# One slot of a cross-attention and routed feed-forward kernel, its parts put in another order on four engines

## The chip, the cores and the metric

The kernel runs on one core of a Trainium2 chip. Every engine has its own program, and semaphores tie them together: TensorE (PE; its weight loads are PEld), VectorE (DVE), ScalarE (ACT), GpSimd (POOL) and SyncE (SP, which here only starts DMAs). The metric is the device time of one execution in microseconds (us); less is better.

## The reference, cut to what matters

Shapes: x and ctx are (128, 128, 256) float32: 128 batches of 128 tokens with 256 features; 16 heads of 16.

```python
def layer(x, ctx):
    q = layernorm(x) @ Wq + bq
    k, v = split(ctx @ Wkv + bkv)
    attn = softmax(q k^T / 4, axis=2)            # over the queries
    x1 = x + (attn v) @ Wo + bo
    y = layernorm(x1)
    keep = top 96 of the 128 tokens of each batch by y @ w_router
    return x1 + where(keep, gelu(y @ w_block), y)
```

## The kernel before, in words

A batch is one tile of 128 tokens by 256 features, and the main loop has one slot s per batch. In a slot each engine works on several batches at different stages, in an order written out by hand; nothing schedules it at run time but the semaphore waits. LEAD is 8. Names in the profile leave out buffer numbers, so x1_sb is shown as x_sb and rstd1 and rstd2 as rstd.

- PE, slot s: `scores(s)` (into ps_s); `transpose_inputs(s+8)` (the normalised input xhat and the context c_sb, into ps_t); `values(s-1)`; `queries_or_keys(s)`, the quarter of the queries or keys of the next four batches, into all of ps_q; `projection(s-2)`; `block_product(s-4)` into ps_t; `transpose_x1(s-3)` into the first half of ps_q; `attention(s-1)`. ps_t is shared by the input transposes and the block product, ps_q by the queries or keys and the transposed x1. So `transpose_x1(s-3)` waits until DVE has read the queries or keys of its own slot (q_raw_ready or k_ready).
- ACT: `x1_high(s-4)`, half of the last quarter of the exponentials of s-1, `attention_copy(s-2)`, the other half, `gelu_tanh(s-7)`, `inputs_high(s+8)`, and the exponentials of s in quarters 3, 2, 1.
- DVE: `x1_low(s-4)`, `maxima(s, 3)` and `(s, 2)`, `values_and_bias(s-1)`, `inputs_low(s+8)`, `inverse_sums_01(s-1)`, `maxima(s, 1)`, `queries` or `keys` (reads ps_q), `residual(s-2)`, `maxima(s, 0)`, `inverse_sums_23(s)`, `final(s-16)`, one `stats` of a pair (the input's in even slots, x1's in odd ones), `product_scaled(s-4)` (reads ps_t). The `router` steps for a group of eight batches lie in five slots of eight.
- POOL: `normalise(s+9)`, in odd slots `rstd1_of_pair(s+11)`, in even slots `rstd2_of_pair(s-4)`, `gelu_square(s-5)`, `values_over_sums(s-1)` (needs `inverse_sums_01(s-1)`, gives v_pad to the attention), `scale_and_shift` in one slot of eight, `unprocessed(s-16)` (gives u_ready to DVE's `final(s-16)`), then `gelu_factor`, `gelu_sum`, `input_and_bias`, `gelu_cubic`, `gelu_product`.

The two waits that the prediction speaks of most are these, one on PE and one on DVE:

```python
# transpose_x1(b), slot = b + 3, quad = slot // 4 * 4 + 4
pe.wait_ge((q_raw_ready, k_ready)[slot % 4 // 2], quad + 2 + slot % 2 * 2)
# final(b), for a batch whose unprocessed part POOL makes
dve.wait_ge(u_ready, b + 1 - u_on_act(b))
```

Of the kernel before, what the change touches and what calls it, by code (L numbers as in the profile page):

```python
# [6 lines left out]
def cross_attention_routed_ffn(  # L7
# [43 lines left out]
    with ctx:  # L51
# [93 lines left out]
        def has(b):  # L145
            return 0 <= b < B

        def upto(b):
            return min(b + 1, B)
# [83 lines left out]
        def _(sp):  # L233
# [63 lines left out]
            load_c(6)  # L297
            load_x(10)
            load_x(12)
            load_x(14)  # L300
            load_c(8)
            load_c(10)
            queries_even_odd_of_pair(2)
            load_c(12)
            load_c(14)
            queries_even_odd_of_pair(4)
            load_x(16)
            queries_even_odd_of_pair(6)

            for s in range(3, B + 18):  # L310
# [12 lines left out]
        def _(pe):  # L323
# [73 lines left out]
            def transpose_inputs(b, settled=False):  # L397

                if not has(b):
                    return  # L400
                if not settled:
                    inputs_ready(b)
                if has(b - LEAD - 5):
                    pe.wait_ge(z_ready, upto(b - LEAD - 5))
                elif 2 <= b <= 4:
                    pe.wait_ge(t_lo_ready, upto(b - 2))
                elif b > 4:
                    pe.wait_ge(t_lo_ready, upto(b - 1))
# [63 lines left out]
            def block_product(b, settled=False):  # L472

                if not has(b):
                    return
                if not settled:
                    pe.wait_ge(xt_ready, upto(b))
                pe.wait_ge(t_lo_ready, upto(b + LEAD + 4))
                if has(b - 1) and not has(b + LEAD + 4):
                    pe.wait_ge(z_ready, upto(b - 1))  # L480
                if b == 0:
                    pe.wait_ge(w_z_lo_ready, 1)
                three_terms(ps_z,
                            lambda a, c: (xt_hi, xt_lo)[a][:, b % 2, c * T:(c + 1) * T],
                            lambda a, c: (w_z_hi, w_z_lo)[a][:, c, :]).then_inc(z_mm, 1)
# [81 lines left out]
            for s in range(2, B - 1):  # L567
                sure = 20 <= s < B - 8
                scores(s)
                if s < 4:  # L570
                    transpose_inputs(2 * s + 4)
                else:
                    transpose_inputs(s + LEAD, s > 4)
                values(s - 1)
                if s < 4:
                    queries_or_keys_of_pair(2 * s, 1)
                else:
                    queries_or_keys(s)
                keep_columns(s - 16)
                candidates(s - 12)  # L580
                projection(s - 2, sure)
                queries_and_keys_ready(s + 1)
                if s < 4:
                    transpose_inputs(2 * s + 5)
                if s == 2:
                    queries_or_keys_of_pair(6, 0)
                if s >= 4:
                    inputs_ready(s + LEAD + 1)
                block_product(s - 4, sure)
                if sure:  # L590
                    scaled_values_ready(s - 1)
                transpose_x1(s - 3, sure)
                router_bank_free(s + 1)
                attention(s - 1, sure)

            scores(B - 1)
            values(B - 2)
            projection(B - 3)
            block_product(B - 5)
            transpose_x1(B - 4)  # L600
            values(B - 1)
            attention(B - 2)
# [15 lines left out]
        def _(act):  # L618
# [108 lines left out]
            for s in range(2, B):  # L727
                sure = 20 <= s < B - 1
                x1_high(s - 4, sure)
                exps(s - 1, 0, halves=(0,))  # L730
                attention_copy(s - 2, sure)
                exps(s - 1, 0, halves=(1,))
                gelu_tanh(s - 7)
                inputs_high(s + LEAD if s >= 4 else 2 * s + 4)
                exps(s, 3, sure)
                exps(s, 2)
                if s < 4:
                    inputs_high(2 * s + 5)
                exps(s, 1)
                if s == 2:  # L740
                    block_weights_high()
# [29 lines left out]
        def _(dve):  # L771
# [156 lines left out]
                        dve.wait_ge(v_pad_ready, upto(b - 2))  # L928
                    nc.vector.tensor_tensor(v_sb[:, b % 2, :], ps_v, bv_sb[:, :], ALU.add).then_inc(v_ready, 1)  # L929

            def product_scaled(b, settled=False):

                if has(b):
                    dve.wait_ge(z_mm, upto(b))
                    if not settled:
                        dve.wait_ge(rstd2_ready, upto(b))
# [96 lines left out]
            for s in range(2, B):  # L1033
                sure = 20 <= s < B - 1
                x1_low(s - 4)
                if s == 3:
                    block_weights_low()
                router(s - 13, 2)
                router(s - 14, 4)
                router(s - 15, 6)  # L1040
                router(s - 16, 8)
                maxima(s, 3)
                maxima(s, 2)
                router(s - 16, 9)
                values_and_bias(s - 1, sure)
                inputs_low(s + LEAD if s >= 4 else 2 * s + 4)
                inverse_sums_01(s - 1)
                maxima(s, 1)
                if s < 4:
                    keys_of_pair(2 * s)  # L1050
# [8 lines left out]
                if s < 4:  # L1059
                    inputs_low(2 * s + 5)  # L1060
                if s == 2:
                    queries_of_pair(6)
                if s == B - 1:
                    values_and_bias(B - 1)
                router(s - 12, 1)
                router(s - 13, 3)
                router(s - 14, 5)
                router(s - 15, 7)
                inverse_sums_23(s)
                final(s - 16, sure)  # L1070
                stats2_of_pair(s - 3)
                if s >= 4:
                    stats1_of_pair(s + 12)
                product_scaled(s - 4, sure)
                if s < 4:
                    stats1_of_pair(2 * s + 8)

# [41 lines left out]
        def _(pool):  # L1119
# [9 lines left out]
            nc.gpsimd.memset(q_eo[:, 1, :, :, :, :], 0.0).then_inc(q_eo_zero, 1)  # L1129

            def rstd1_of_pair(b):

# [125 lines left out]
            normalise(5)  # L1258
            input_and_bias(0)
            input_and_bias(1)  # L1260
            rstd1_of_pair(6)
            normalise(6)
            normalise(7)
# [6 lines left out]
            for s in range(2, 4):  # L1270
# [5 lines left out]
            rstd1_of_pair(14)  # L1276

            for s in range(4, B):
                sure = 20 <= s < B - 1
                normalise(s + LEAD + 1, sure)  # L1280
                rstd1_of_pair(s + 11)
                rstd2_of_pair(s - 4)
                gelu_square(s - 5, sure)
                values_over_sums(s - 1, sure)
                scale_and_shift(s - 16)
                unprocessed(s - 16, sure)
                gelu_factor(s - 5)
                gelu_sum(s - 7)
                input_and_bias(s + 2)
                gelu_cubic(s - 5)  # L1290
                gelu_product(s - 7)

            rstd2_of_pair(B - 4)
            gelu_factor(B - 5)
            scale_and_shift(B - 16)
            values_over_sums(B - 1)
# [41 lines left out]
```

## Time and profile before

| | |
|---|---|
| time, median of 3 runs | 902.11 us (901.8 to 902.36) |
| the profiled execution: its own time, its span | 904.1 us, 902.3 us |
| busy share of the span: PE, PEld | 96%, 80% |
| DVE, ACT, POOL | 95%, 96%, 88% |
| granted clock of TensorE, mean | 0.991 of full speed (2.4 GHz) |
| DMA | 70.40 MB, mean 78 GB/s |

The busy shares are taken over the whole span, with a start and an end that are less full than the middle. The durations in the timeline reach from an instruction's start to its end and overlap with the next one's; what an instruction costs its engine is the distance from its start to the next start. Below that is called its spacing.

### The profile page before, as it was taken

The numbers are of one execution on the slowest core, as the hardware profiler recorded it, in microseconds if no ns is written. First come the engines' busy times: TensorE is split into PE (matmuls) and PEld (weight loads), VectorE is DVE, ScalarE is ACT, GpSimd is POOL, SyncE is SP. The second block draws the span as 40 slices with busy tenths as digits, with TensorE's granted clock in tenths as the row PEclk, the third lists the DMA queues.
The fourth block names the chain that finished last, engine by engine and source line by source line (L and its number), as shares of the span: only waits on it lengthen the run. The fifth ranks groups of instructions, "written<-read, shape, count | busy, mean of one in ns | idle before, by whom it ended". The sixth has DMA issues, their size and how long they took to land. (4 is left out here: it accounts for less than half of the span.)

```text
span 902.3 us, 30174 instructions
## 1 busy us (share of the span) xinstructions
PE 864.8 (96%) x9842; PEld 718.8 (80%) x9842; DVE 857.9 (95%) x2068; ACT 870.6 (96%) x4632; POOL 789.6 (88%) x1489
## 2 busy tenths in 40 slices
PE   6999999999999999999999999999999999999972
PEld 6778888888888888888888888888888888888752
DVE  5888999999999999999999999999999999999987
ACT  4999999999999999999999999999999999999984
POOL 5468879999999999999999999999999999998865
PEclk9999999999999999999999999999999999999997
DMA  7221123232323232223333222323222323211102
GB/s 233 69 65 53 54 63 86 79 93 59 84 82 89 72 96 69 79 79 85 84 83 91 57 80 88 91 72 95 61 85 79 87 78 90 75 40 40 41 24 94
DMA packets 71357, 70.40 MB, mean 78 GB/s; under 512 B 12064, under 2 KB 63520, under 8 KB 71200
## 3 DMA queue, kind: packets, MB, share of 16 engines
q1 hardware_dynamic: 69840, 67.68, 26.4%
q8 instruction: 79, 1.29, 0.6%
q10 hardware_dynamic: 1360, 0.79, 0.3%
q14 instruction: 78, 0.64, 0.2%
HBM read 35.13 MB, written 16.78 MB: 58 GB/s over the span
## 5 line engine op out<-in xcount | busy, mean ns | idle before, releaser
L646 ACT ACTIVATE e_sb<-ps_s,neg_max 128x128 f32<-128x128 f32 x2048 | 772.1, 639 | 2.8 <-DVE neg_max L805 2.7
L646 ACT ACTIVATION_READ_ACCUMULATOR e_sb<-ps_s,neg_max 128x1 f32 x2048 | 718.2, 464 | 0.0
L805 DVE TENSOR_REDUCE neg_max<-ps_s 128x4 f32<-128x512 f32 x512 | 331.0, 666 | 19.7 <-PE ps_s L385 18.2
L385 PE MATMUL ps_s<-q_eo,k_sb 32*128 32x256 f32 x2048 | 146.6, 399 | 3.6 <-ACT e_sb L646 1.5
L450 PE MATMUL ps_a<-e_sb,v_pad 128*32 128x128 f32 x4096 | 138.4, 276 | 1.5 <-POOL v_pad L1168 0.9
L344 PE MATMUL ps_a<-w_o_sb,o_sb 128*128 128x256 f32 x512 | 131.7, 379 | 4.0 <-DVE v_sb L929 3.8
L450 PEld LDWEIGHTS ps_a<-e_sb,v_pad 128*32 128x32 f32 x4096 | 104.1, 109 | 23.2 <-issue 21.5
L385 PEld LDWEIGHTS ps_s<-q_eo,k_sb 32*128 32x128 f32 x2048 | 95.8, 184 | 32.9 <-issue 28.7
L344 PEld LDWEIGHTS ps_a<-w_o_sb,o_sb 128*128 128x128 f32 x512 | 93.8, 189 | 22.8 <-issue 4.7
L1157 POOL TENSOR_TENSOR x_sb<-x_sb,bo_sb 128x256 f32<-128x256 f32 x128 | 105.1, 822 | 0.2
L1168 POOL TENSOR_TENSOR v_pad<-v_sb,recip 128x256 f32<-128x256 f32 x128 | 79.5, 621 | 29.1 <-DVE recip L865 27.1
L657 ACT CAST t_hi<-ps_t 128x512 fp32r<-128x512 f32 x126 | 94.3, 748 | 7.5 <-PE ps_t L414 7.0
L688 ACT ACTIVATE g_sb<-g_sb 128x256 f32<-128x256 f32 x128 | 99.0, 774 | 1.4 <-POOL g_sb L1215 1.4
L337 PE MATMUL ps_t<-w_z_hi,xt_hi 128*128 128x258 f32 x256 | 96.4, 377 | 2.2 <-DVE z_sb L941 2.2
L665 ACT COPY o_sb<-ps_a 128x256 f32<-128x256 f32 x128 | 91.1, 712 | 2.4 <-PE ps_a L450 2.4
L633 ACT CAST xt_hi<-ps_q 128x256 fp32r<-128x256 f32 x128 | 88.4, 691 | 1.4 <-PE ps_q L430 1.4
L1215 POOL TENSOR_TENSOR g_sb<-g_sb,z_sb 128x256 f32<-128x256 f32 x128 | 88.3, 690 | 0.3
L873 DVE TENSOR_TENSOR t_lo<-ps_t,t_hi 128x512 fp32r<-128x512 f32 x126 | 85.2, 676 | 2.7 <-ACT t_hi L657 2.6
L337 PE MATMUL ps_a<-w_v_hi,t_hi 128*128 128x256 f32 x256 | 83.2, 325 | 0.7 <-DVE w_z_sb L797 0.7
L1229 POOL TENSOR_TENSOR z_sb<-g_sb,z_sb 128x256 f32<-128x256 f32 x121 | 82.8, 684 | 0.0
L1198 POOL TENSOR_TENSOR g_sb<-z_sb 128x256 f32<-128x256 f32 x123 | 75.3, 612 | 0.0
L337 PE MATMUL ps_a<-w_v_lo,t_hi 128*128 128x256 f32 x256 | 72.5, 283 | 0.0
(113 smaller groups left out, 2213.8 us busy)
## 6 DMA issues: line engine op xcount, KB each, us to landing
x_sb<-in_x SPq DMA_DIRECT2D x64, 256.0 KB, 3.0
c_sb<-in_ctx SPq DMA_DIRECT2D x64, 256.0 KB, 3.0
out<-z_sb SPq DMA_DIRECT2D x64, 256.0 KB, 2.4
q_eo<-q_raw SPq DMA_DIRECT2D x504, 32.0 KB, 2.0
z_sb<-in_L_xattn_Wkv ACTq DMA_DIRECT2D x2, 256.0 KB, 6.7
z_sb<-in_L_xattn_Wq ACTq DMA_DIRECT2D x1, 256.0 KB, 3.6
w_z_sb<-in_L_ffn_w_block SPq DMA_DIRECT2D x1, 256.0 KB, 8.0
w_o_sb<-in_L_xattn_Wo SPq DMA_DIRECT2D x1, 256.0 KB, 7.1
```

The source lines that it names most:

```text
L337: last = nc.tensor.matmul(dst, lhs(a, c), rhs(b, c), start=(c == 0 and n == 0), stop=(c == C - 1 and n == len(terms) - 1))
L344: last = nc.tensor.matmul(dst, lhs(c), rhs(c), start=(c == 0), stop=(c == C - 1))
L385: mm = nc.tensor.matmul(ps_s[:, bank(b, j), c, :, :], k_sb[rows, r2, c, h * T:(h + 1) * T], q_eo[rows, r2, :, c, h, :], start=True, stop=True)
L450: mm = nc.tensor.matmul(ps_attn[32 * j:32 * j + 32, c * T:(c + 1) * T], v_pad[:, b % 2, c * J + j, par:par + 2, :].rearrange("p a d -> p ( ...
L633: nc.scalar.copy(xt_hi[:, b % 2, :], ps_xt).then_inc(xt_hi_ready, 1)
L646: last = nc.scalar.activation(e_sb[:, b % 3, j, c, par, :], ps_s[:, bank(b, j), c, par, :], ACT.Exp, bias=neg_max[:, b % 4, h:h + 1], accu ...
L657: nc.scalar.copy(t_hi[:, n, :, :, h * T:(h + 1) * T].rearrange("p k c t -> p (k c) t"), inputs_bank(b)[:, :].rearrange("p (n t) -> p n t", ...
L665: nc.scalar.copy(o_sb[:, b % 2, :], ps_attn).then_inc(o_ready, 1)
L688: nc.scalar.activation(g_sb[:, b % 4, :], g_sb[:, b % 4, :], ACT.Tanh, scale=SLOPE).then_inc(tanh_ready, 1)
L805: nc.vector.tensor_reduce(neg_max[:, b % 4, :].rearrange("p (c j q) -> p j c q", c=C, j=J)[:, j, :, :], ps_s[:, bank(b, j), :, :, :], AX.X ...
L1157: nc.gpsimd.tensor_tensor(x_sb[:, b % RX, :], x_sb[:, b % RX, :], bo_sb[:, :], ALU.add).then_inc(xb_ready, 1)
L1215: nc.gpsimd.tensor_tensor(g_sb[:, b % 4, :], g_sb[:, b % 4, :], z_sb[:, b % R, 0:E], ALU.mult).then_inc(cubic_ready, 1)
```

## The change: what it does

It moves parts within the slot, and adds or removes no arithmetic.

- PE: `transpose_inputs(s+8)` goes from behind the scores to behind `transpose_x1(s-3)`, and `block_product(s-4)` from there to behind the values. Their two waits for the shared ps_t are moved on by one batch.
- ACT: `inputs_high` is now that of batch s+7, behind `x1_high`; the last quarter of the exponentials of s-1 is no longer cut in two by the attention's copy.
- DVE: `inputs_low(s+7)` behind `x1_low`; `product_scaled(s-4)` behind `inverse_sums_01(s-1)`.
- POOL: `values_over_sums(s-1)` is first. `rstd1_of_pair` is now in even slots, and `rstd2_of_pair` is in odd ones, behind `input_and_bias`.
- At the start SP waits for one weight before four of its loads and puts two x loads later, a memset of POOL comes later, and in the last slots the block product has its new place as well.

```diff
@@ the PE loop
                 scores(s)
                 if s < 4:
                     transpose_inputs(2 * s + 4)
-                else:
-                    transpose_inputs(s + LEAD, s > 4)
                 values(s - 1)
+                block_product(s - 4, sure)
...
                 projection(s - 2, sure)
                 queries_and_keys_ready(s + 1)
-                if s < 4:
-                    transpose_inputs(2 * s + 5)
+                if s >= 4:
+                    inputs_ready(s + LEAD)
+                transpose_x1(s - 3, sure)
+                transpose_inputs(s + LEAD if s >= 4 else 2 * s + 5, s >= 4)
+                router_bank_free(s + 1)
+                attention(s - 1)
...
-                block_product(s - 4, sure)
-                if sure:
-                    scaled_values_ready(s - 1)
-                transpose_x1(s - 3, sure)
-                router_bank_free(s + 1)
-                attention(s - 1, sure)
@@ its waits
-                if has(b - LEAD - 5):
-                    pe.wait_ge(z_ready, upto(b - LEAD - 5))
+                if has(b - LEAD - 4):
+                    pe.wait_ge(z_ready, upto(b - LEAD - 4))
...
-                pe.wait_ge(t_lo_ready, upto(b + LEAD + 4))
+                pe.wait_ge(t_lo_ready, upto(b + LEAD + 3))
@@ the ACT loop
                 x1_high(s - 4, sure)
-                exps(s - 1, 0, halves=(0,))
+                if s == 3:
+                    inputs_high(9)
+                elif s >= 4:
+                    inputs_high(s + LEAD - 1)
                 attention_copy(s - 2, sure)
-                exps(s - 1, 0, halves=(1,))
+                exps(s - 1, 0)
                 gelu_tanh(s - 7)
-                inputs_high(s + LEAD if s >= 4 else 2 * s + 4)
@@ the DVE loop
                 x1_low(s - 4)
...
+                elif s >= 4:
+                    inputs_low(s + LEAD - 1)
...
                 values_and_bias(s - 1, sure)
-                inputs_low(s + LEAD if s >= 4 else 2 * s + 4)
...
                 inverse_sums_01(s - 1)
+                product_scaled(s - 4)
...
-                product_scaled(s - 4, sure)
@@ the POOL loop
+                values_over_sums(s - 1, sure)
                 normalise(s + LEAD + 1, sure)
-                rstd1_of_pair(s + 11)
-                rstd2_of_pair(s - 4)
+                rstd1_of_pair(s + 10)
                 gelu_square(s - 5, sure)
-                values_over_sums(s - 1, sure)
                 scale_and_shift(s - 16)
                 unprocessed(s - 16, sure)
                 gelu_factor(s - 5)
                 gelu_sum(s - 7)
                 input_and_bias(s + 2)
+                rstd2_of_pair(s - 3)
```

PE, one slot of the middle of the program, the first matmul of each group and what it waits for (the rest of a group stands behind it). First before:

```order
L385 MATMUL ps_s<-q_eo,k_sb 128x256 [waits exp_ready1,recip_23_ready]
L414 MATMUL ps_t<-ident,xhat 128x128 [waits z_ready]
L337 MATMUL ps_a<-w_v_hi,t_hi 128x256 [waits o_ready]
L337 MATMUL ps_q<-t_hi,w_k_hi 128x512 [waits xt_ready]
L344 MATMUL ps_a<-w_o_sb,o_sb 128x256 [waits v_ready]
L337 MATMUL ps_t<-w_z_hi,xt_hi 128x258 [waits c_in6,t_lo_ready,xhat_ready,q_eo_in1]
L430 MATMUL ps_q<-ident,x1_sb 128x128 [waits k_ready,v_pad_ready]
L450 MATMUL ps_a<-e_sb,v_pad 32x128 [waits x1_ready]
```

And the same slot of the change:

```order
L386 MATMUL ps_s<-q_eo,k_sb 128x256 [waits exp_ready1,recip_23_ready]
L338 MATMUL ps_a<-w_v_hi,t_hi 128x256 [waits o_ready]
L338 MATMUL ps_t<-w_z_hi,xt_hi 128x258 [waits t_lo_ready]
L338 MATMUL ps_q<-t_hi,w_k_hi 128x512 [waits xt_ready]
L345 MATMUL ps_a<-w_o_sb,o_sb 128x256 [waits v_ready]
L431 MATMUL ps_q<-ident,x1_sb 128x128 [waits k_ready,xhat_ready,q_eo_in1]
L415 MATMUL ps_t<-ident,xhat 128x128 [waits z_ready]
L451 MATMUL ps_a<-e_sb,v_pad 32x128 [waits x1_ready,v_pad_ready]
```

The block product (ps_t with w_z) has left the place between the projection (w_o) and the transposed x1, whose first matmul waits for k_ready.

POOL, from the scaled values (v_pad, L1168) to the unprocessed part (x_sb with alpha and beta, L1247) in two slots running, before:

```order
L1168 TENSOR_TENSOR v_pad<-v_sb,recip 128x8x2x16 [waits recip_ready]
L1247 TENSOR_SCALAR x_sb<-x_sb,alpha,beta 128x256 [waits beta_ready]
L1208 TENSOR_SCALAR g_sb<-g_sb 128x256 [waits square_ready]
L1222 TENSOR_SCALAR g_sb<-g_sb 128x256 [waits tanh_ready]
L1157 TENSOR_TENSOR x_sb<-x_sb,bo_sb 128x256 [waits xhat_ready]
```

And of the change, in an even slot:

```order
L1166 TENSOR_TENSOR v_pad<-v_sb,recip 128x8x2x16 [waits recip_ready]
L1146 TENSOR_SCALAR xhat<-x_sb,neg_m,rstd 128x256 [waits rstd1_r]
L1134 TENSOR_SCALAR ve<-st 128x2 [waits st1_r]
L1135 TENSOR_SCALAR neg_m<-st 128x2
L1137 TENSOR_TENSOR rstd<-ve,minus_half 128x2 [waits ve1_r]
L1196 TENSOR_TENSOR g_sb<-z_sb 128x256 [waits z_ready]
L1245 TENSOR_SCALAR x_sb<-x_sb,alpha,beta 128x256 [waits beta_ready]
L1206 TENSOR_SCALAR g_sb<-g_sb 128x256 [waits square_ready]
```

The normalised input, three small operations and the square now lie between the scaled values and the unprocessed part, which nothing separated before.

## Rows read from the trace of the kernel before

**Rows 1.** Busy time by engine in 80 us of the middle (busy, instructions; TensorE clock, DMA)

```profile
480.00:560.00 80.00, 79.66 (x915) 66.29 (x914) 79.20 (x199) 80.00 (x434) 75.07 (x141) 1.00 0.28 81
```

**Rows 2.** Timeline of PE, scores of slots 16 and 120: start, us, engine, line, operation

```profile
128.02 1.15 PE L385 MATMUL ps_s<-q_eo,k_sb 32*128 32x256 f32 x16
...
823.82 1.15 PE L385 MATMUL ps_s<-q_eo,k_sb 32*128 32x256 f32 x16
```

**Rows 3.** Timeline of PE, slot 6: scores, last keys, block product, transposed x1, next scores

```profile
61.47 1.15 PE L385 MATMUL ps_s<-q_eo,k_sb 32*128 32x256 f32 x16
...
64.91 0.39 PE L337 MATMUL ps_q<-t_lo,w_k_hi 128*128 128x512 f32 x1
...
65.81 0.47 PE L337 MATMUL ps_t<-w_z_hi,xt_hi 128*128 128x258 f32 x1
66.12 0.28 PE L337 MATMUL ps_t<-w_z_hi,xt_lo 128*128 128x258 f32 x1
...
66.72 0.38 PE L430 MATMUL ps_q<-ident,x_sb 128*128 128x128 f32 x2
...
68.04 1.15 PE L385 MATMUL ps_s<-q_eo,k_sb 32*128 32x256 f32 x16
```

**Rows 4.** Timeline of PE and of DVE: queries in slot 3, and who waited for them

```profile
39.15 0.28 PE L337 MATMUL ps_q<-t_lo,w_q_hi 128*128 128x256 f32 x1
...
39.53 0.69 DVE L886 TENSOR_TENSOR q_raw<-ps_q,bq_sb 128x512 f32<-128x512 f32 x1 [0.17 <-PE ps_q L337]
```

**Rows 5.** Timeline of DVE, from one final to the next and a later one

```profile
509.10 0.72 DVE L994 SCALAR_TENSOR_TENSOR z_sb<-z_sb,half_keep,x_sb 128x256 f32<-128x256 f32 x1
509.74 0.69 DVE L851 BATCH_NORM_STATS2 st<-x_sb 128x6 f32<-128x512 f32 x1
510.36 0.46 DVE L941 TENSOR_SCALAR z_sb<-ps_t,rstd 128x258 f32<-128x258 f32 x1
510.74 0.41 DVE L818 TENSOR_TENSOR xt_lo<-ps_q,xt_hi 128x256 fp32r<-128x256 f32 x1
511.07 1.27 DVE L805 TENSOR_REDUCE neg_max<-ps_s 128x4 f32<-128x512 f32 x2
...
513.23 0.19 DVE L865 RECIPROCAL recip<-sums 128x8 f32<-128x8 f32 x1
...
513.90 0.74 DVE L910 TENSOR_SCALAR q_raw<-ps_q,bq_sb 128x512 f32<-128x512 f32 x1
...
515.60 0.63 DVE L994 SCALAR_TENSOR_TENSOR z_sb<-z_sb,half_keep,x_sb 128x256 f32<-128x256 f32 x1
...
522.17 0.51 DVE L994 SCALAR_TENSOR_TENSOR z_sb<-z_sb,half_keep,x_sb 128x256 f32<-128x256 f32 x1
522.60 0.69 DVE L851 BATCH_NORM_STATS2 st<-x_sb 128x6 f32<-128x512 f32 x1
```

**Rows 6.** Timeline of POOL, around the unprocessed part (L1247) of two slots

```profile
508.03 0.21 POOL L1237 TENSOR_TENSOR beta<-drop_rstd,st 128x8 f32<-128x8 f32 x1 [0.61 <-DVE half_keep L978]
...
508.51 0.55 POOL L1247 TENSOR_SCALAR x_sb<-x_sb,alpha,beta 128x256 f32<-128x256 f32 x1
509.14 0.40 POOL L1208 TENSOR_SCALAR g_sb<-g_sb 128x256 f32<-128x256 f32 x1
...
511.96 0.56 POOL L1148 TENSOR_SCALAR xhat<-x_sb,neg_m,rstd 128x256 f32<-128x256 f32 x1
512.60 0.19 POOL L1136 TENSOR_SCALAR ve<-st 128x2 f32<-128x2 f32 x1
...
513.73 0.61 POOL L1198 TENSOR_TENSOR g_sb<-z_sb 128x256 f32<-128x256 f32 x1
...
514.91 0.56 POOL L1247 TENSOR_SCALAR x_sb<-x_sb,alpha,beta 128x256 f32<-128x256 f32 x1
```

**Rows 7.** Groups by line of DVE, the router's rounds: count, busy us, mean ns

```profile
L967 DVE MAX8 top<-cand 8x8 f32<-8x128 f32 x64 | 17.5, 273 | 0.4
L961 DVE MATCH_REPLACE8 cand<-top,cand 8x128 f32<-8x128 f32 x64 | 16.9, 264 | 0.0
```

More of the change, by code:

```diff
@@ L299, in _ @@
             load_x(12)
-            load_x(14)
+            sp.wait_ge(w_in["v"], 16)
             load_c(8)
@@ L303, in _ @@
             queries_even_odd_of_pair(2)
+            load_x(14)
+            queries_even_odd_of_pair(4)
             load_c(12)
+            load_x(16)
             load_c(14)
-            queries_even_odd_of_pair(4)
-            load_x(16)
             queries_even_odd_of_pair(6)
@@ L477, in block_product @@
                     pe.wait_ge(xt_ready, upto(b))
-                pe.wait_ge(t_lo_ready, upto(b + LEAD + 4))
-                if has(b - 1) and not has(b + LEAD + 4):
+                pe.wait_ge(t_lo_ready, upto(b + LEAD + 3))
+                if has(b - 1) and not has(b + LEAD + 3):
                     pe.wait_ge(z_ready, upto(b - 1))
@@ L582, in _ @@
                 queries_and_keys_ready(s + 1)
-                if s < 4:
-                    transpose_inputs(2 * s + 5)
+                if s >= 4:
[4 more added lines that the diff above has]
+                attention(s - 1)
                 if s == 2:
                     queries_or_keys_of_pair(6, 0)
-                if s >= 4:
-                    inputs_ready(s + LEAD + 1)
-                block_product(s - 4, sure)
-                if sure:
-                    scaled_values_ready(s - 1)
-                transpose_x1(s - 3, sure)
-                router_bank_free(s + 1)
-                attention(s - 1, sure)
             scores(B - 1)
             values(B - 2)
+            block_product(B - 5)
             projection(B - 3)
-            block_product(B - 5)
             transpose_x1(B - 4)
@@ L729, in _ @@
                 x1_high(s - 4, sure)
-                exps(s - 1, 0, halves=(0,))
+                if s == 3:
+                    inputs_high(9)
+                elif s >= 4:
+                    inputs_high(s + LEAD - 1)
                 attention_copy(s - 2, sure)
-                exps(s - 1, 0, halves=(1,))
+                exps(s - 1, 0)
                 gelu_tanh(s - 7)
-                inputs_high(s + LEAD if s >= 4 else 2 * s + 4)
+                if s < 4:
+                    inputs_high(2 * s + 4)
                 exps(s, 3, sure)
                 exps(s, 2)
-                if s < 4:
-                    inputs_high(2 * s + 5)
                 exps(s, 1)
@@ L929, in values_and_bias, with product_scaled @@
                     nc.vector.tensor_tensor(v_sb[:, b % 2, :], ps_v, bv_sb[:, :], ALU.add).then_inc(v_ready, 1)
-            def product_scaled(b, settled=False):
+            def product_scaled(b):
                 if has(b):
                     dve.wait_ge(z_mm, upto(b))
-                    if not settled:
-                        dve.wait_ge(rstd2_ready, upto(b))
+                    dve.wait_ge(rstd2_ready, upto(b))
                     if b % 2 == 0 and has(b - R):
@@ L1037, in _ @@
                     block_weights_low()
+                    inputs_low(9)
+                elif s >= 4:
+                    inputs_low(s + LEAD - 1)
                 router(s - 13, 2)
@@ L1045, in _ @@
                 values_and_bias(s - 1, sure)
-                inputs_low(s + LEAD if s >= 4 else 2 * s + 4)
+                if s < 4:
+                    inputs_low(2 * s + 4)
                 inverse_sums_01(s - 1)
+                product_scaled(s - 4)
                 maxima(s, 1)
@@ L1058, in _ @@
                 maxima(s, 0)
-                if s < 4:
-                    inputs_low(2 * s + 5)
                 if s == 2:
@@ L1128, in _ @@
             nc.gpsimd.memset(q_eo[:, 0, :, :, 2:4, :], 0.0).then_inc(q_eo_zero, 1)
-            nc.gpsimd.memset(q_eo[:, 1, :, :, :, :], 0.0).then_inc(q_eo_zero, 1)
             def rstd1_of_pair(b):
@@ L1260, in _ @@
             input_and_bias(1)
+            nc.gpsimd.memset(q_eo[:, 1, :, :, :, :], 0.0).then_inc(q_eo_zero, 1)
             rstd1_of_pair(6)
@@ L1275, in _ @@
                 input_and_bias(s + 2)
-            rstd1_of_pair(14)
+            rstd2_of_pair(0)
             for s in range(4, B):
                 sure = 20 <= s < B - 1
+                values_over_sums(s - 1, sure)
                 normalise(s + LEAD + 1, sure)
-                rstd1_of_pair(s + 11)
-                rstd2_of_pair(s - 4)
+                rstd1_of_pair(s + 10)
                 gelu_square(s - 5, sure)
-                values_over_sums(s - 1, sure)
                 scale_and_shift(s - 16)
@@ L1289, in _ @@
                 input_and_bias(s + 2)
+                rstd2_of_pair(s - 3)
                 gelu_cubic(s - 5)
                 gelu_product(s - 7)
-            rstd2_of_pair(B - 4)
             gelu_factor(B - 5)
```

## The prediction

> **What bounds the kernel now.** I read the busy time of a stretch in the middle first. ACT is busy all 80.00 of 80 us, PE 79.66, DVE 79.20 and POOL 75.07 [rows 1]: four engines within 7% of each other, so a gain on one can't pass the next, while a wait put on any of them can soon be a loss. Then the pace. From the scores of slot 16 to those of slot 120 it takes 695.80 us [rows 2], 104 slots or 13 rounds of eight (the router's period): 6.69 us a slot, 53.52 a round. With ACT never idle, that is ACT's work. Slot 6, early, before ACT has all of its work, takes 6.57 [rows 3], with PE's matmuls end to end: that is PE's own need. For DVE I added spacings along one slot, and found that it is nearly as full as ACT (below). So the question to ask of each moved part is which wait it puts on PE, DVE or POOL, and not what it saves.
>
> **PE: the block product.** It now stands behind the values. It opened with a matmul 0.31 us from its second, where its others stand 0.12 apart [rows 3]; behind the values, which are of the same kind, I expect 0.12, a saving of 0 to 0.19. But it also was the cover of a wait. The transposed x1 goes into ps_q, and must let DVE read the queries or keys there first. Before, it started 1.81 us behind the last matmul of the keys; the block product began at 0.90 [rows 3], and there the transposed x1 stands now. What it needs: the matmul's 0.39, then 0.10 until DVE starts (39.43 to 39.53 [rows 4]), DVE's 0.74 [rows 5], and a handover for which I take POOL to DVE, 0.04 (509.06 to 509.10 [rows 5, 6]): 1.27. So PE stands still for 0.37 in each slot with queries or keys, even when DVE is there in time. PE's slot becomes 6.57 + 0.37 - 0.19 = 6.75, or 6.94 if nothing is saved. The moved input transposes cost what they did, as far as any row tells. I take 6.85, the middle: already above ACT's 6.69.
>
> **POOL and DVE: the unprocessed part.** This is the larger term. DVE's final of a batch needs POOL's unprocessed part. Before, that stood directly behind the scaled values. Now the normalised input, in even slots the three operations of its statistic, and the square come between. I count from DVE's reciprocal that the scaled values need.
> - POOL's way in an even slot: the reciprocal's 0.19 [rows 5] and a handover of 0.04; normalised input and statistic 1.77 (511.96 to 513.73); square and scaled values 1.18 (513.73 to 514.91); the unprocessed part 0.56 [rows 6]; a handover of 0.04. Sum 3.78.
> - DVE's way to the same final: reciprocal and maxima 0.67 (513.23 to 513.90), the scaled product, now here, 0.38 (510.36 to 510.74), then queries, residual, maxima and reciprocal 1.70 (513.90 to 515.60) [rows 5]. Sum 2.75. So DVE stands at final for 1.03 us. The wait for the queries' matmuls lies inside this stretch and is hidden by it: PE's 6.85 leaves DVE 0.56 to wait at most, by DVE's 6.29 below.
> - From final to the next slot's reciprocal: final itself; statistics 0.62; x1's low half 0.33; then two maxima, values and the inputs' low half 2.16 (511.07 to 513.23) [rows 5]. That is 3.11 besides final.
>
> Final took 0.64 where it started right behind the unprocessed part, 0.04 before POOL's next operation (509.10 against 509.14), and 0.43 in a later slot [rows 5, 6]. In the even slots of the change each final starts right behind the unprocessed part, so 0.64 is the row nearest to it. The Trainium skill (SBUF — State Buffer, Who interferes with whom) says that a VectorE instruction with two SBUF inputs and a GpSimd instruction that reads SBUF can't run together: the later one waits. By that rule the 0.64 is what every such meeting costs, and the rows agree with it; if all finals took 0.43 instead, the sum below would be 11 us less.
>
> An even slot is then 3.78 + 0.64 + 3.11 = 7.53 us on DVE. An odd slot has no such wait: without the statistic's 1.13 (512.60 to 513.73 [rows 6]) POOL needs 2.65, less than DVE's 2.75. It is 2.75 + 0.43 + 3.11 = 6.29, or 6.50 with a slow final; I take 6.4. Who waits for a late DVE: PE, whose next transposed x1 needs the queries read, and ACT, whose exponentials need the maxima. So the pair costs 13.93 where PE alone would allow 13.70, and a round 55.7.
>
> Two more things lie on this way. The router's rounds, 17.5 + 16.9 us for 16 groups [rows 7], are 2.15 a round of eight slots. The two of its MAX8 that stand between reciprocal and final in even slots vanish in the wait (2 x 0.27), so 1.6 counts. And beta and alpha, once a round and in an even slot, add 0.48 ahead of the unprocessed part (508.03 to 508.51 [rows 6]). A round is 55.7 + 1.6 + 0.5 = 57.8 against 53.52: **4.3 us more, and 56 over 13 rounds.** In the other 16 slots with queries or keys (4 to 15, no unprocessed part yet, and 120 to 123) I count PE's 6.85 against some 6.65: 3 us.
>
> **What costs nothing.** ACT's converted inputs are now made at the start of the slot from transposes that stand a whole attention ahead of it, so its wait there goes; but ACT was busy all the time [rows 1], and what is late next is DVE. The exponentials joined into one quarter are the same instructions. The scaled product earlier on DVE is counted above; PE's input transposes no longer wait for it last. The scaled values' first place on POOL brings nothing, since their reciprocal decides, and the attention that needs them comes last in PE's slot. x1's statistic, now late in odd slots, is wanted a slot later. The start (SP's wait for a weight, two loads issued later, a memset moved) I bound by 2 us either way, some 0.12 a slot, the 6.69 less 6.57 of rows 2 and 3, for 16 slots, and take at nothing.
>
> **The sum.** 56 + 3 = 59. The profiled execution took 904.1 us with a span of 902.3, and stands 2.0 above the median of 902.1. The difference goes onto the median: 902 + 59 = 961.
>
> **The rivals.**
> - *PE's wait alone.* If POOL's unprocessed part is in time after all, because POOL starts its slot earlier or DVE arrives later by itself, the slot is PE's 6.85: 120 slots x 0.16 = 19 us, 921; with 6.94, 932. For it: only a second of the two engines has to be 1.03 us off my count. Against it: the count is made of plain spacings.
> - *The waits add up.* If DVE's wait for the queries isn't covered by POOL's way, because the reciprocal moves with it, each even slot costs up to 0.56 more: 13 x 4 x 0.56 = 29 us, 990. Against it: the reciprocal stands ahead of the queries.
> - *Not slower.* PE saves 0.19 and its transposes no longer stand behind DVE's scaled product. If DVE's read of the queries ended within the 0.90 that are left, and final met no wait, ACT's 6.69 would go on bounding the slot, and with a smoother start the time is 900 to 902. The point that decides is a way through DVE of 0.90 where I count 1.27, and 2.75 for POOL where I count 3.78. Faster by more than 2 us it can't be, since ACT is full.
>
> **How the numbers follow.** The forecast, 940 to 980, gets 0.60. PE's wait alone gets 0.18, the added waits above 980 get 0.12. Not slower gets 0.10, half of it within 0.2% (about what a measurement of this kernel tells from no change), half of it faster. The range goes from 921, PE's wait alone at its middle, to 980; it leaves out the case that isn't slower, most of the added waits and a little of the second case, some 0.2 together. So faster 0.05, same 0.05, slower 0.90.
>
> **What would show it.** In the profile after, ACT should be busy less than 95% of the middle. DVE's final should wait for POOL's unprocessed part by about 1 us in even slots, most in the one with beta. PE's transposed x1 should wait for DVE's queries or keys in every slot. The scores should stand some 57.8 us apart over eight slots, uneven, with slots of 6.4 to 6.9 after slots of 7.5 and more. The forecast is wrong if ACT is still full, if final shows no wait, or if the transposed x1 starts within 1 us of the last keys' matmul.

## The result, and the profile after

The changed kernel takes **967.11 us** (median of 4 runs, 965.74 to 967.82), the kernel before 902.24 (901.8 to 902.62): a ratio of 1.0717, 95% interval 1.0699 to 1.0736. The forecast was 961 with a range of 921 to 980, so sign and size came out. The profiled execution took 965.74 us with a span of 963.9, 61.6 more than the span of before.

Busy time of the same 80 us as in [rows 1] (PE, PEld, DVE, ACT, POOL, with the number of instructions; then TensorE's clock, DMA share, GB/s):

```profile
480.00:560.00 80.00, 76.16 (x839) 59.58 (x838) 74.06 (x173) 74.29 (x396) 68.59 (x132) 1.00 0.28 77
```

ACT fell from 80.00 to 74.29, and every other engine fell with it. No engine took over as the bound: all of them now wait. The clock is granted in full, so nothing of the loss lies there.

The scores of slots 16 and 120 in the timeline of PE, as in [rows 2]:

```profile
129.43 1.15 PE L386 MATMUL ps_s<-q_eo,k_sb 32*128 32x256 f32 x16
...
884.20 1.15 PE L386 MATMUL ps_s<-q_eo,k_sb 32*128 32x256 f32 x16
```

They are 754.77 us apart, 58.06 a round, where it was 695.80 and 53.52. So 58.97 of the 61.6 us were lost in these 104 slots. Slots 4 to 15 lost another 3.43 (83.14 against 79.71 from the scores of slot 4 to those of slot 16), and the rest about cancels: the profiled execution starts 2.8 sooner, and slots 0 to 3 and 120 to 127 take some 2 more.

Who waits, from the table of waits between 200 and 760 us (engine, what it wrote, who released it: us in total, times, longest):

```profile
POOL v_pad L1166 <- DVE recip L863: 52.0, 47, 1.4
ACT e_sb L642 <- DVE neg_max L803: 28.0, 38, 1.2
...
DVE z_sb L991 <- POOL x_sb L1245: 21.4, 37, 1.3
...
PEld ps_t L338 <- DVE t_lo L871: 15.5, 37, 1.0
```

Read the third row shown first: DVE's final (L991) waits for POOL's unprocessed part (L1245). DVE is late after that, so POOL waits for the next reciprocal (L863) and ACT for the maxima (L803). The same table of the kernel before, which goes down to sums of 0.9 us, has none of these three.

One even slot without the router's shift on DVE, from reciprocal to reciprocal, with what POOL does in it (start, us, engine, line, operation, and in brackets the idle time before and its releaser):

```profile
554.36 0.19 DVE L863 RECIPROCAL recip<-sums 128x8 f32<-128x8 f32 x1
...
555.77 0.75 DVE L916 TENSOR_SCALAR k_sb<-ps_q,bk_sb 128x512 f32<-128x512 f32 x1 [0.27 <-issue]
...
558.20 0.72 DVE L991 SCALAR_TENSOR_TENSOR z_sb<-z_sb,half_keep,x_sb 128x256 f32<-128x256 f32 x1 [0.49 <-POOL x_sb L1245]
...
561.90 0.19 DVE L863 RECIPROCAL recip<-sums 128x8 f32<-128x8 f32 x1
```

```profile
554.63 0.62 POOL L1166 TENSOR_TENSOR v_pad<-v_sb,recip 128x256 f32<-128x256 f32 x1
555.24 0.55 POOL L1146 TENSOR_SCALAR xhat<-x_sb,neg_m,rstd 128x256 f32<-128x256 f32 x1
...
556.33 0.71 POOL L1137 TENSOR_TENSOR rstd<-ve,minus_half 128x2 f32<-128x2 f32 x1
557.01 0.61 POOL L1196 TENSOR_TENSOR g_sb<-z_sb 128x256 f32<-128x256 f32 x1
557.61 0.56 POOL L1245 TENSOR_SCALAR x_sb<-x_sb,alpha,beta 128x256 f32<-128x256 f32 x1
558.25 0.41 POOL L1206 TENSOR_SCALAR g_sb<-g_sb 128x256 f32<-128x256 f32 x1
```

From reciprocal to final it is 3.84 us; POOL fills this with the values, the normalised input, the statistic, the square and the unprocessed part, without a gap worth naming. The slot is 7.54 (554.36 to 561.90). Final waits 0.49 of it. That is less than the 1 us that the prediction named as a sign, because DVE has waited for PE on the way there (0.27 for the keys in the row of L916, some 0.15 at the projection), a wait that the prediction had placed inside this stretch.

The odd slot before it, from reciprocal to reciprocal (547.76 to 554.36), and PE's projection in it:

```profile
547.76 0.19 DVE L863 RECIPROCAL recip<-sums 128x8 f32<-128x8 f32 x1
...
549.65 0.42 DVE L825 TENSOR_TENSOR x_sb<-ps_a,x_sb 128x256 f32<-128x256 f32 x1
...
550.71 0.43 DVE L991 SCALAR_TENSOR_TENSOR z_sb<-z_sb,half_keep,x_sb 128x256 f32<-128x256 f32 x1
...
552.82 1.29 DVE L803 TENSOR_REDUCE neg_max<-ps_s 128x4 f32<-128x512 f32 x2
```

```profile
548.59 1.02 PE L345 MATMUL ps_a<-w_o_sb,o_sb 128*128 128x256 f32 x4
```

It takes 6.60: 2.95 to final, 0.35 for final, 3.30 to the next reciprocal. Final waits for nothing here. But DVE follows PE at two places: the residual (L825) starts right behind the projection (549.61), and the maxima (L803) start behind the scores' matmuls, which end at 552.68.

And PE's slot 6, as in [rows 3], before the router starts:

```profile
60.15 1.15 PE L386 MATMUL ps_s<-q_eo,k_sb 32*128 32x256 f32 x16
...
62.04 0.28 PE L338 MATMUL ps_t<-w_z_hi,xt_hi 128*128 128x258 f32 x1
62.16 0.28 PE L338 MATMUL ps_t<-w_z_hi,xt_lo 128*128 128x258 f32 x1
...
63.91 0.39 PE L338 MATMUL ps_q<-t_lo,w_k_hi 128*128 128x512 f32 x1
...
65.29 0.41 PE L431 MATMUL ps_q<-ident,x_sb 128*128 128x128 f32 x2
...
67.08 1.15 PE L386 MATMUL ps_s<-q_eo,k_sb 32*128 32x256 f32 x16
```

The block product now opens with the plain distance of 0.12, so its 0.19 is saved. The transposed x1 starts 1.38 behind the start of the last matmul of the keys, though nothing of PE's lies there but the projection. The slot is 6.93, and it was 6.57.

### The profile page after: what moved, and what is told of

Read it like the earlier page. It is cut to its first block and busy times, and to the rows that moved or that the text cites. A ratio compares the mean times of both kernels' runs of the same rounds, so it can differ in the third digit from the quotient of the medians.

```text
span 963.9 us, 30180 instructions
## 1 busy us (share of the span) xinstructions
PE 899.5 (93%) x9842; PEld 706.8 (73%) x9842; DVE 882.2 (92%) x2068; ACT 882.4 (92%) x4632; POOL 785.1 (81%) x1489
## 5 line engine op out<-in xcount | busy, mean ns | idle before, releaser
L642 ACT ACTIVATE e_sb<-ps_s,neg_max 128x128 f32<-128x128 f32 x2048 | 692.6, 444 | 39.9 <-DVE neg_max L803 39.5
L642 ACT ACTIVATION_READ_ACCUMULATOR e_sb<-ps_s,neg_max 128x1 f32 x2048 | 540.3, 269 | 0.0
L803 DVE TENSOR_REDUCE neg_max<-ps_s 128x4 f32<-128x512 f32 x512 | 336.1, 676 | 12.1 <-PE ps_s L386 8.1
L386 PEld LDWEIGHTS ps_s<-q_eo,k_sb 32*128 32x128 f32 x2048 | 92.9, 184 | 31.2 <-issue 24.1
L991 DVE SCALAR_TENSOR_TENSOR z_sb<-z_sb,half_keep,x_sb 128x256 f32<-128x256 f32 x128 | 71.9, 566 | 31.4 <-POOL x_sb L1245 31.1
L1155 POOL TENSOR_TENSOR x_sb<-x_sb,bo_sb 128x256 f32<-128x256 f32 x128 | 92.8, 725 | 0.2
L338 PE MATMUL ps_t<-w_z_hi,xt_hi 128*128 128x258 f32 x256 | 78.2, 305 | 13.7 <-DVE t_lo L871 10.5
L338 PEld LDWEIGHTS ps_a<-w_v_hi,t_hi 128*128 128x128 f32 x256 | 48.1, 188 | 42.5 <-issue 42.0
L431 PEld LDWEIGHTS ps_q<-ident,x_sb 128*128 128x128 f32 x256 | 26.0, 140 | 67.5 <-issue 43.4
L431 PE MATMUL ps_q<-ident,x_sb 128*128 128x128 f32 x256 | 52.4, 286 | 21.7 <-DVE q_raw L908 7.9
```

Of the source, the lines that this page charges most:

```text
L338: last = nc.tensor.matmul(dst, lhs(a, c), rhs(b, c), start=(c == 0 and n == 0), stop=(c == C - 1 and n == len(terms) - 1))
L386: mm = nc.tensor.matmul(ps_s[:, bank(b, j), c, :, :], k_sb[rows, r2, c, h * T:(h + 1) * T], q_eo[rows, r2, :, c, h, :], start=True, stop=True)
L642: last = nc.scalar.activation(e_sb[:, b % 3, j, c, par, :], ps_s[:, bank(b, j), c, par, :], ACT.Exp, bias=neg_max[:, b % 4, h:h + 1], accu ...
L803: nc.vector.tensor_reduce(neg_max[:, b % 4, :].rearrange("p (c j q) -> p j c q", c=C, j=J)[:, j, :, :], ps_s[:, bank(b, j), :, :, :], AX.X ...
L1155: nc.gpsimd.tensor_tensor(x_sb[:, b % RX, :], x_sb[:, b % RX, :], bo_sb[:, :], ALU.add).then_inc(xb_ready, 1)
```

## The experiments

Each kernel was timed against the kernel before on the same chip (903.45 us for the first four, 902.11 for the last three). "Round" is the distance of the scores of slots 16 and 120 divided by 13, as above.

### POOL's unprocessed part directly behind the values

```diff
                 values_over_sums(s - 1, sure)
+                scale_and_shift(s - 16)
+                unprocessed(s - 16, sure)
                 normalise(s + LEAD + 1, sure)
...
                 gelu_square(s - 5, sure)
-                scale_and_shift(s - 16)
-                unprocessed(s - 16, sure)
```

> The changed kernel, but GpSimd does the router's scale and shift and the unprocessed sum directly behind the values, ahead of the normalising, the square root and the square. Theory (GpSimd's order makes most of the loss): the final sum's wait of 0.5 us in plain even slots and 1.3 us in those with the router's shift goes; what is left is TensorE's slot of 6.92 us, so a round of eight falls from 58.2 to some 55.5 us and the time from 967 to about 930 us (918 to 942). Rival (GpSimd's order is harmless and TensorE's order and VectorE's moved work make the loss): within 3 us of 967.

Measured: 939.0 us, ratio 1.0391 (1.0376 to 1.0407), inside the theory's range. The round is 55.87. The waits for the same stretch of time, those that speak of POOL, DVE and PE:

```profile
PEld ps_q L431 <- issue: 33.5, 63, 0.8
...
POOL v_pad L1166 <- DVE recip L863: 9.4, 27, 0.9
```

Final's wait for the unprocessed part is gone from the table, ACT's for the maxima too, and so is PE's for `t_lo`. POOL's order is shown to cost 28 us, 13 rounds of 2.19. What is left is a slot of 6.92 to 6.96 in seven of the eight places of a round (the eighth takes 7.3): PE's, with the transposed x1 standing still. That is the first row; "issue" means that the view names no releaser.

### PE's inputs ahead of x1

```diff
-                transpose_x1(s - 3, sure)
                 transpose_inputs(s + LEAD if s >= 4 else 2 * s + 5, s >= 4)
                 router_bank_free(s + 1)
+                transpose_x1(s - 3, sure)
```

> The changed kernel, but TensorE transposes the inputs of a later item ahead of x1 instead of behind it, so that some 0.57 us of its own work lies between the last keys or queries and the transpose that waits for VectorE to read them. Theory (two separate costs, TensorE's wait of 0.3 to 0.4 us per slot and GpSimd's order in even slots): the slots that now take 6.92 us fall to about 6.6, the even slots stay bound by the unprocessed sum, so the time falls by 5 to 15 us, to 952 to 962. Rival (TensorE's wait sets every slot): eight times 0.3 us per round, about 2.4 us in each of 15 rounds, to about 930.

Measured: 963.34 us, ratio 1.066 (1.0645 to 1.0676), just above the theory's 962 and far from the rival's 930. Slots 4 to 15 fell from 6.92 to between 6.63 and 6.75, which gives 3.4 us (from the scores of slot 4 to those of slot 16, 79.76 against 83.14). But the round is 57.98 against 58.06: where the unprocessed part exists, the edit is worth next to nothing. Its rows show why, from one reciprocal of an odd slot to the next of an even one, and that one's final:

```profile
545.05 0.18 DVE L863 RECIPROCAL recip<-sums 128x8 f32<-128x8 f32 x1
...
551.39 0.19 DVE L863 RECIPROCAL recip<-sums 128x8 f32<-128x8 f32 x1
...
555.44 0.72 DVE L991 SCALAR_TENSOR_TENSOR z_sb<-z_sb,half_keep,x_sb 128x256 f32<-128x256 f32 x1 [0.76 <-POOL x_sb L1245]
```

```profile
551.17 0.74 POOL L1227 TENSOR_TENSOR z_sb<-g_sb,z_sb 128x256 f32<-128x256 f32 x1
551.86 0.62 POOL L1166 TENSOR_TENSOR v_pad<-v_sb,recip 128x256 f32<-128x256 f32 x1
```

The odd slot is 6.34 now instead of 6.60. But at 551.39 POOL is still at the last operation of the odd slot, so the values start 0.47 behind the reciprocal instead of 0.27, and final comes after 4.05 instead of 3.84. What PE and DVE gain in the odd slot, POOL's own work takes back in the even one. The loop is POOL's odd slot, its even slot as far as the unprocessed part, and DVE from final to the next reciprocal; PE has no part in it. So it goes in two of a round's four pairs of slots. In the other two the odd slot holds steps of the router, takes 6.6 and 7.2 in both kernels, and has nothing to gain.

### Both

The two edits above together.

> Both edits at once: GpSimd's unprocessed sum directly behind the values and TensorE's inputs ahead of x1. Theory: neither wait is left, the slot is ScalarE's or TensorE's 6.6 to 6.7 us as in the kernel before, and the earlier start of 2 us is kept: 897 to 906 us. Rival (a third cost lies in VectorE's own moved work, the scaled product ahead of the maxima and the low parts of the inputs early in the slot): 910 to 930.

Measured: 916.95 us, ratio 1.0154 (1.0138 to 1.0171), in the rival's range. The round is 54.47. The edit on PE, worth 3.8 us alone, is worth 22 once the unprocessed part is early (939.0 to 916.95). So the two waits don't add up: PE's is hidden as long as POOL's is there. Still 13.5 us are missing to the kernel before. Busy time in the middle, as in [rows 1]:

```profile
480.00:560.00 80.00, 79.73 (x908) 65.39 (x907) 79.29 (x192) 79.25 (x424) 74.35 (x140) 1.00 0.29 81
```

DVE is busy 79.29 of 80, for a round that is 0.95 longer than before: its instructions take longer from start to start. But not those that the rival names: the scaled product takes 433 ns in the mean against 461 before, and the low half of the inputs 673 against 675. Two groups of DVE between 200 and 760 us, before and in this kernel (busy us, mean ns | idle before):

```profile
L994 DVE SCALAR_TENSOR_TENSOR z_sb<-z_sb,half_keep,x_sb 128x256 f32<-128x256 f32 x84 | 41.5, 494 | 1.1
L972 DVE TENSOR_SCALAR keep_row<-cand 8x128 f32<-8x128 f32 x10 | 2.1, 208 | 0.0
```

```profile
L991 DVE SCALAR_TENSOR_TENSOR z_sb<-z_sb,half_keep,x_sb 128x256 f32<-128x256 f32 x82 | 45.5, 555 | 2.2
L969 DVE TENSOR_SCALAR keep_row<-cand 8x128 f32<-8x128 f32 x10 | 4.6, 462 | 0.0
```

Eight finals a round at 61 ns more are 0.49, one keep_row is 0.25: 0.74 of the 0.95. Both are longer by whatever POOL runs beside them (see the last section). By the distances from start to next start, without the idle time that the view lists, the two make 0.64 a round between the scores of slots 16 and 120. The rest moved both ways: the maxima take 0.54 more, queries and keys 0.45, the reciprocals 0.25; the scaled product and x1's low half take 0.57 less, and listed idle time fell by 0.40. So the 0.95 is a balance, and the longer finals are its cause only as far as these rows tell: no run took them away. Nor did a run test the rival that the waits of this kernel offer: POOL now stands 1.1 once a round for the router's half_keep (10.8 us between 200 and 760 us, 5.5 before), and PE's attention then waits for the values (3.3 us).

### POOL's order alone, in the kernel before

```diff
             for s in range(4, B):
                 sure = 20 <= s < B - 1
+                values_over_sums(s - 1, sure)
                 normalise(s + LEAD + 1, sure)
-                rstd1_of_pair(s + 11)
-                rstd2_of_pair(s - 4)
+                rstd1_of_pair(s + 10)
                 gelu_square(s - 5, sure)
-                values_over_sums(s - 1, sure)
...
                 input_and_bias(s + 2)
+                rstd2_of_pair(s - 3)
```

The statistics ahead of the loop and behind it move along, and DVE's scaled product now waits for x1's statistic by itself, as in the change; no such wait shows in its table.

> The kernel before, with the changed kernel's order of GpSimd alone: values first, then the normalising, the square roots and the square, and only then the unprocessed sum. Theory (GpSimd's order makes most of the loss): the final sum on VectorE waits in the even slots and the round grows from 53.5 to 57 to 60.5 us, 945 to 995 us. Rival (the order is harmless where TensorE and VectorE keep theirs): 902, within 3 us.

Measured: 1006.22 us, ratio 1.1139 (1.1123 to 1.1156), outside what either theory said: more than the whole change costs. The round is 61.15. An even slot with the router's shift, on DVE, and who stands behind it on PE, ACT and POOL:

```profile
568.24 0.72 DVE L994 SCALAR_TENSOR_TENSOR z_sb<-z_sb,half_keep,x_sb 128x256 f32<-128x256 f32 x1 [1.71 <-POOL x_sb L1247]
```

```profile
570.02 0.44 PE L414 MATMUL ps_t<-ident,xhat 128*128 128x128 f32 x2 [1.29 <-DVE z_sb L941]
```

```profile
570.71 0.59 ACT L657 CAST t_hi<-ps_t 128x512 fp32r<-128x512 f32 x1 [1.61 <-PE ps_t L414]
```

```profile
572.64 0.62 POOL L1168 TENSOR_TENSOR v_pad<-v_sb,recip 128x256 f32<-128x256 f32 x1 [1.53 <-DVE recip L865]
```

In the old order DVE's scaled product stands behind final, PE's input transposes stand right behind the scores and wait for it, and ACT waits for those. So a late final passes through DVE, PE and ACT on its way back to POOL. With the change's other moves (the scaled product early on DVE, the transposes late on PE) the same order of POOL gives 967. So they are worth 39 us where final is late; where it is in time, as in the first kernel above, they come with PE's wait and leave the kernel 36 us above the kernel before.

This kernel also bears on the start. Its loads are those of the kernel before, and its first scores stand at 15.07 us; with the change's start they stand at 14.53 in the change and at 14.90 to 15.29 in the six other kernels here, and in the profiled execution of before at 17.29. So most of the 2.8 us by which the change seems to start sooner isn't the change's.

### The old order of the normalising, with the new rest

```diff
-                values_over_sums(s - 1, sure)
                 normalise(s + LEAD + 1, sure)
                 rstd1_of_pair(s + 10)
                 gelu_square(s - 5, sure)
+                values_over_sums(s - 1, sure)
                 scale_and_shift(s - 16)
```

> The changed kernel, but GpSimd does the normalising, the square root and the square ahead of the values, as in the kernel before; TensorE's and VectorE's new orders stay. Theory (what costs is work of GpSimd between the values and the unprocessed sum): the same gain as with the unprocessed sum directly behind the values, so slots of 6.92 us throughout, set by TensorE's wait for the keys or queries to be read: 930 to 940. Rival (the place of the values early in GpSimd's slot also matters, for the attention or for the normalising): over 945 or under 925.

Measured: 943.94 us, ratio 1.046 (1.0442 to 1.0478); the round is 56.32. The theory's upper end was 940, and the runs lie above it, just below the rival's 945. Then the same with PE's inputs ahead of x1, the edit shown for the second kernel:

> The same, and TensorE transposes the inputs ahead of x1. Theory (with the unprocessed sum directly behind the values TensorE set 6.93 us a slot, without the waits VectorE is full and sets 54.5 us a round, 1.0 over the kernel before, some of it because the final sum took 0.9 us beside GpSimd's square): with the square gone from beside the final sum the round comes to 53.6 to 54.2, the time to 904 to 914. Rival (VectorE's own order costs the 1.0 us): 915 to 919, as with both edits before.

Measured: 940.7 us, ratio 1.0424 (1.0409 to 1.044); the round is 56.25. A miss for both theories. The waits of this second kernel, in the same stretch:

```profile
POOL ve L1177 <- DVE st L832: 41.2, 39, 1.1
...
PE ps_a L451 <- POOL v_pad L1166: 18.9, 40, 0.6
DVE z_sb L991 <- POOL x_sb L1245: 17.3, 40, 0.8
```

The first of them is new. The change has moved the statistic of x1 into the odd slot, behind `input_and_bias`. It needs what DVE computes behind its final of the same slot; in the kernel before it stood a slot later. With the values behind the normalising and the square, POOL gets to it about 1 us before DVE does, stands there, and starts its even slot late; final waits again, 40 times (20 times in the first of the two kernels). So, by these waits, POOL is again in the loop in both kernels, and with it PE's edit is again worth nothing in the round (56.25 against 56.32).

### POOL's neighbour of final

```diff
                 unprocessed(s - 16, sure)
+                input_and_bias(s + 2)
                 gelu_factor(s - 5)
                 gelu_sum(s - 7)
-                input_and_bias(s + 2)
                 rstd2_of_pair(s - 3)
```

> The changed kernel, but GpSimd adds the bias to a later input directly behind the unprocessed sum, and does the gelu's factor and sum behind that. Theory (the even slots are a chain through the unprocessed sum and the final sum, and the final sum takes 0.64 us instead of 0.42 because of the neighbour on GpSimd): the final sum takes 0.42 us everywhere and the round falls by three or four times 0.2 us, so 955 to 960. Rival (the neighbour does not set it, or the 0.2 us are given back in the next wait): within 3 us of 967.

Measured: 978.41 us, ratio 1.0841 (1.0825 to 1.0858); the round is 58.98. A miss for both, with the other sign than the theory's: the neighbour does set final's time, but this one makes it longer. An even slot of this kernel, on POOL and on DVE:

```profile
520.27 0.56 POOL L1245 TENSOR_SCALAR x_sb<-x_sb,alpha,beta 128x256 f32<-128x256 f32 x1
520.79 0.73 POOL L1155 TENSOR_TENSOR x_sb<-x_sb,bo_sb 128x256 f32<-128x256 f32 x1
```

```profile
520.86 0.94 DVE L991 SCALAR_TENSOR_TENSOR z_sb<-z_sb,half_keep,x_sb 128x256 f32<-128x256 f32 x1 [0.17 <-POOL x_sb L1245]
```

Final starts 0.07 behind POOL's next operation and ends 0.28 after that one's end (521.52 to 521.80). In the change the neighbour is shorter (0.41), and final takes 0.72. Four finals a round at 0.22 more are 0.88, and the round grew by 0.92. In the kernel before the same neighbour did no harm, as these rows show:

```profile
482.32 1.01 POOL L1157 TENSOR_TENSOR x_sb<-x_sb,bo_sb 128x256 f32<-128x256 f32 x1
```

```profile
482.33 0.42 DVE L994 SCALAR_TENSOR_TENSOR z_sb<-z_sb,half_keep,x_sb 128x256 f32<-128x256 f32 x1
```

There it was final that went through, and POOL's operation that took 1.01 instead of 0.73. I had taken the 0.42 for a property of the neighbour; it belongs to the one of the two that goes first.

## Why the prediction was right, point by point

**What bounds it.** Four engines within 7% of each other, so that a wait put on one becomes a loss: so it was. ACT is busy 93% of the middle.

**PE.** The saving of 0.19 came in full. The way through DVE, taken as 1.27, is 1.38 in slot 6: DVE's read of the keys starts at 64.40 and takes 0.75, so what I had too small is the handover from DVE to PE, 0.14 where I took POOL's to DVE of 0.04. So PE stands 0.48 and not 0.37. Another 0.07 came on top, nearly all of it in the moved input transposes and the transposed x1, 0.78 together where they took 0.72; I had put that at nothing. The slot is 6.93. With the whole saving my own sum was 6.75, so that 6.85 is so near is partly the luck of having taken the middle. For the slots outside the routed stretch I counted 3 us; slots 4 to 15 alone gave 3.43.

**POOL and DVE.** The way to final in an even slot is 3.84 (taken 3.78) and with the router's shift 4.28 (3.78 + 0.48). Final's spacing is 0.65 (558.20 to the statistics at 558.85; taken 0.64), and from its end to the next reciprocal it is 3.05 (taken 3.11). The even slot is 7.54, and I had 7.53. The term that was too small is the odd slot: 6.60 where I took 6.4. I had DVE's waits for PE hidden. In the odd slot they stand in the open: 2.95 to final instead of 2.75, most of it at the projection, and 3.30 behind final instead of 3.11, at the scores. Final itself was short, 0.35 where I took 0.43 to 0.64. With PE's inputs ahead of x1 only the wait at the scores goes, and the odd slot is 2.93 + 0.35 + 3.06 (545.05 to 551.39); that this comes near my 6.29 is luck. The router and its shift add some 1.5 a round to four pairs of 14.14, where I took 2.1: part of its steps fill DVE's waits for PE in the odd slots too. So a round is 58.06 against the 57.8 of the text because 0.8 too little in the odd slots stands against 0.6 too much for the router. 13 rounds cost 59.0 instead of 56.

**The sum.** 59 was forecast. The spans differ by 61.6, the medians by 64.9. The profiled execution of before stands 1.9 over the median of 902.24, that of after 1.4 under its own, which accounts for the 3.3 between the two. Of the 5.9 us between 59 and 64.9, 3 lie in the rounds; 1.9 in the slots outside them that I counted with 3 (3.43 in slots 4 to 15, 1.43 in slots 120 to 123); 0.7 in the first four slots, which I had taken at nothing.

**What I did not name.** PE's block product, now early in the slot, waits for DVE's low half of the inputs: 0.8 us at its longest on PE. It is a consequence of the late final: the wait is absent where the unprocessed part is early (the first and the third kernel).

**The rivals.** "PE's wait alone" (921 to 932) is what the kernel with the early unprocessed part shows, at 939, 7 us above its range: the mechanism is there and worth 22 us, but it lies below the larger one. "The waits add up" is excluded for the even slots, where DVE's wait for the keys lies inside the 3.84, and by the second and third kernels: the waits overlap. In the odd slots a part of DVE's waits for PE did show, as said. "Not slower" would have needed both ways to be shorter, and with both shortened the kernel still takes 917.

**Where the cause is shown and where argued.** That POOL's order costs 28 us, and PE's wait another 22 below it, is shown by taking each away. The 13.5 that are left are only read from the rows of DVE, and their cause stays open. The moves of ACT, of DVE and of the start were not tried by themselves.

## What to carry to other kernels

Where two engines hand work back and forth, follow the loop: here unprocessed part, final, next reciprocal, next values. An operation put ahead of the one that another engine waits for lengthens that way by its full duration, and costs what the other engine's own way doesn't cover: the 2.37 us put ahead of the unprocessed part in an even slot (555.24 to 557.61) left final a wait of 0.49. And everything outside the loop can be improved nearly without effect until the loop is cut. So take the longest wait away first, and judge a second edit only on top of that: the same move on TensorE was worth 4 us before and 22 after. And an order of one engine belongs to the orders of the others: POOL's alone in the old kernel cost 103 us, together with the change's other moves 65.

## What the hardware showed that I had not expected

I expected that final is slowed by a fixed 0.2 us beside some of POOL's operations. The rows read as if one of the two waits out the other whole. Where final is the one that waits, it ends 0.26 to 0.30 us behind the end of POOL's operation: 0.72 beside one of 0.41, 0.94 beside one of 0.73. Two operations of POOL in a row can be waited out together. The kernel with both edits, on POOL and on DVE:

```profile
480.05 0.56 POOL L1146 TENSOR_SCALAR xhat<-x_sb,neg_m,rstd 128x256 f32<-128x256 f32 x1
480.57 0.62 POOL L1196 TENSOR_TENSOR g_sb<-z_sb 128x256 f32<-128x256 f32 x1
```

```profile
480.55 0.92 DVE L991 SCALAR_TENSOR_TENSOR z_sb<-z_sb,half_keep,x_sb 128x256 f32<-128x256 f32 x1
```

Final begins at 480.55, when POOL's first operation is nearly at its end, and isn't let in between the two: it ends at 481.47, 0.28 after the second (481.19). That happens to 13 finals of this kernel after 150 us; 13 others, which start 0.01 to 0.03 before the end of a small operation of POOL (neg_m), are let in. So is the final of before at 482.33 above: POOL's earlier operation ends at 482.35, and the one behind it waits. What decides between the two stays open.

The Trainium skill (SBUF — State Buffer, Who interferes with whom) says that the order of issue, and not the shape of an operation, decides who blocks. The traces agree that the shape doesn't: the same final beside the same operation of POOL took 0.42 and 0.94. The order can't be read from the recorded starts where these lie within some 0.1 us of each other: at 558.20 final starts 0.05 ahead of POOL's next operation and is the one that waits, at 482.33 it starts 0.01 behind it and goes through. One thing held in these two kernels: where final had been waiting for the unprocessed part, POOL's very next operation went first, in all 49 such meetings of the change after 150 us, and in all 50 of the kernel with the other neighbour. It isn't a rule. In the kernel with POOL's order alone POOL went first in the 50 cases in which final had waited 0.83 or more, and final in the 11 in which it had waited 0.15, as here:

```profile
513.67 0.70 POOL L1208 TENSOR_SCALAR g_sb<-g_sb 128x256 f32<-128x256 f32 x1
```

```profile
513.62 0.48 DVE L994 SCALAR_TENSOR_TENSOR z_sb<-z_sb,half_keep,x_sb 128x256 f32<-128x256 f32 x1 [0.15 <-POOL x_sb L1247]
```

So final, once released by an operation of POOL, meets the one behind it. Where final has waited long, that one's length sets the price; where it comes at the same moment, either can win.

Even the small keep_row of 8 partitions, 0.21 in the mean in the kernel before, takes 0.64 in the change, behind an operation of POOL of 0.74:

```profile
480.50 0.74 POOL L1227 TENSOR_TENSOR z_sb<-g_sb,z_sb 128x256 f32<-128x256 f32 x1
```

```profile
480.68 0.64 DVE L969 TENSOR_SCALAR keep_row<-cand 8x128 f32<-8x128 f32 x1
```
